# Layout of the stored values: by head instead of by token tile, stored two tiles at a time

## The chip, the cores and the metric

The kernel runs on one core of a Trainium2 chip. The metric is device time in microseconds, the median of several runs. TensorE (PE) multiplies, VectorE (DVE), ScalarE (ACT) and GpSimd (POOL) work on elements, and SyncE (SP) issues nearly all transfers, which sixteen DMA engines carry out.

## The reference

One transformer layer over 2 sequences of 1024 tokens, width 512, 16 heads of 32. Attention and the mixture of experts both read the same normalized input.

```python
xn = _layernorm(x, axis=-1)
Q, K, V = split_heads(xn @ Wq.T), split_heads(xn @ Wk.T), split_heads(xn @ Wv.T)
S = where(causal, einsum('bhqd,bhkd->bhqk', Q, K) * scale, -1e30)
attn = (softmax(S) @ V).transpose(0, 2, 1, 3).reshape(b, t, D) @ Wo.T
routed = sum over the 2 chosen of 8 experts: weight * (silu(xn @ gw.T) * (xn @ uw.T)) @ dw.T
x + attn + routed + shared_mlp(xn)
```

## The kernel before

All of it is one program in five stages, each a block with a barrier between them: the norm stage (`norm_phase`), the projection of queries and keys (`project_phase`), attention with the shared expert mixed in (`attend_phase`), the output projection, and the routed experts. Large products are done in two parts, hi and lo, whose sum is the fp32 number, so that a stored value of one head has 2 * DK = 64 numbers: 32 hi and 32 lo.

**The norm stage** goes over NT = 16 token tiles of 128 rows. For tile t the steps are: load x (L236), statistics on DVE (L271), normalize on DVE (`scale`, L295), transpose on PE (L386), hi and lo parts of the transposed tile on ACT (L357) and DVE (`lo`, L304), 12 matmuls with the value weights into `ps_v` (L397), hi part of the values on ACT (`v_hi`, L369) and lo part on DVE (`v_lo`, L317), both into `v_stage`, and the store of `v_stage` to memory (`store_v`, L246). The normalized tile is stored too (`store_xn`, L241).

There are four slots for each buffer. The order on each engine is fixed by `pipeline`, which takes a list of (lag, step): in turn t the engine does each step for tile t - lag, in the order of the list. DVE does in one turn invert (lag 1), statistics (0), scale (1), lo (2), aggregate (0), v_lo (4), add_eps (0), save_lo (2). SyncE's list is:

```python
pipeline(sp, NT, U, [(0, load), (0, store_zeros), (3, store_xn), (5, store_v)])
```

So SyncE issues, in turn t, the load of x tile t, the store of normalized tile t - 3, and the store of values of tile t - 5. Each waits for its semaphore, and whatever comes later on SyncE waits behind it. All go to one hardware queue (q1 in the profile), which is a ring on each of the sixteen DMA engines.

`v_hi` waits until the slot that it overwrites has been stored. At the head of the projection stage ACT waits, before its first instruction (L515), until every store of values and of normalized rows has landed.

**Memory layout.** Values go to `v_rows`, of shape [128 partitions, 16 tiles, 16 heads, 64]. The store of a tile is 4096 contiguous bytes for each partition. In the attention stage `load_values` (L939) fetches for each of the 32 (head, sequence) pairs 8 tiles of one head: 8 pieces of 256 bytes for each partition, 4096 bytes apart in memory, which land in `vs` with a gap of two numbers between tiles. `vs` has four slots, and the load for one pair is issued a whole head before PE multiplies with it.

Of the kernel before, what the change touches and what calls it, by code (L numbers as in the profile page):

```python
# [22 lines left out]
F32 = mybir.dt.float32  # L23
# [9 lines left out]
H, DK = 16, 32  # L33
P = 128
# [52 lines left out]
def moe_attention_kernel(nc, x, wqk, wv, wo, router, bias, gate, up, down, sgate, sup, sdown, out):  # L87
    qk_hi = nc.dram_tensor("qk_hi", [2 * D, T], F32, kind="Internal").ap()
    qk_lo = nc.dram_tensor("qk_lo", [2 * D, T], F32, kind="Internal").ap()
    v_dram = nc.dram_tensor("v_rows", [P, NT, H, 2 * DK], F32, kind="Internal").ap()  # L90
    row_dram = nc.dram_tensor("max_rows", [2 * H, S], F32, kind="Internal").ap()
    xn_dram = nc.dram_tensor("xn_rows", [T + P, D], F32, kind="Internal").ap()
    slots_dram = nc.dram_tensor("slots", [NSLOT, 2], F32, kind="Internal").ap()
    xt_dram = nc.dram_tensor("xt_blocks", [NTB, P, 2, KC, TBW], F32, kind="Internal").ap()
    with ExitStack() as ctx:
        ident = ctx.enter_context(nc.sbuf_tensor("ident", [P, P], F32))

        slot_of = ctx.enter_context(nc.sbuf_tensor("slot_of", [P, NT, 2], I32))
        entry = ctx.enter_context(nc.sbuf_tensor("entry", [P, NT, 2, 2], F32))

        slot_table = ctx.enter_context(nc.sbuf_tensor("slot_table", [P, NST, 2], F32))
        expert_of = ctx.enter_context(nc.sbuf_tensor("expert_of", [P, NST], I32))


        work = ctx.enter_context(nc.sbuf_tensor("work", [P, NT, D], F32))
        r_hi = ctx.enter_context(nc.sbuf_tensor("r_hi", [P, KC, E], F32R))
        r_lo = ctx.enter_context(nc.sbuf_tensor("r_lo", [P, KC, E], F32R))

        def counters(name, n):
            return [ctx.enter_context(nc.semaphore(f"{name}{k}")) for k in range(n)]  # L110

        v_stored = counters("v_stored", NORM_SLOTS)
        xn_stored = counters("xn_stored", NORM_SLOTS)
        (zeros_stored,) = counters("edge_stored", 1)
        qk_stored = counters("qk_stored", 2)
        (xt_stored,) = counters("xt_stored", 1)
        y_stored = counters("y_stored", YS)

        rows = ctx.enter_context(nc.sbuf_tensor("rows", [P, ROW_SLOTS], I32))
        rows_ready, experts_ready = counters("routed_input", 2)  # L120
        gathered = counters("gathered", GS)
        expert_loaded = counters("expert_loaded", len(FIRST_AT))
        (passed,) = counters("passed", 1)
        with ExitStack() as shared_ctx:

            shared_w = [tuple(shared_ctx.enter_context(nc.sbuf_tensor(name + part, shape, F32R))
                              for part in ("_hi", "_lo"))
                        for name, shape in (("sg", [P, KC, F]), ("su", [P, KC, F]),
                                            ("sd", [P, len(FCH), D]))]
            chosen, weight, earlier_of = [  # L130
                shared_ctx.enter_context(nc.sbuf_tensor(name, [P, NT, E], F32))
                for name in ("chosen", "weight", "earlier_of")]
            count_of = shared_ctx.enter_context(nc.sbuf_tensor("count_of", [P, 1, E], F32))
            with nc.sbuf_tensor("xt_hi", [P, KC, T], F32R) as xt_hi, \
                    nc.sbuf_tensor("xt_lo", [P, KC, T], F32R) as xt_lo:
                norm_phase(nc, x, wv, xt_hi, xt_lo, ident, v_dram, xn_dram, out, work, v_stored,
                           xn_stored, zeros_stored, router, r_hi, r_lo, passed)
                project_phase(nc, wqk, r_hi, r_lo, bias, xt_hi, xt_lo, ident, chosen, weight,
                              earlier_of, count_of, shared_w, sgate, sup, sdown, qk_hi, qk_lo, work,
                              v_stored + xn_stored, zeros_stored, qk_stored, xt_dram, xt_stored)  # L140
            attend_phase(nc, x, ident, qk_hi, qk_lo, v_dram, row_dram, xt_dram, shared_w, sgate,
                         sup, sdown, chosen, weight, earlier_of, count_of, slot_of, entry,
                         slot_table, expert_of, slots_dram, out, work, qk_stored, xt_stored)

        with nc.sbuf_tensor("gu_sb", [P, E * KC, 2 * F], F32) as gu_sb, \
                nc.sbuf_tensor("d_sb", [P, E * len(FCH), D], F32) as d_sb, \
                nc.sbuf_tensor("y_tile", [P, YS, D], F32) as y_tile:
            out_phase(nc, wo, gate, up, down, ident, work, gu_sb, d_sb, out, y_tile, y_stored,
                      slot_table, rows, rows_ready, xn_dram, gathered, passed, expert_loaded)
            routed_phase(nc, gate, up, down, ident, gu_sb, d_sb, slot_table, expert_of, xn_dram,  # L150
                         work, out, y_stored, rows, rows_ready, gathered, passed, expert_loaded,
                         experts_ready)
# [25 lines left out]
def norm_phase(nc, x, wv, xt_hi, xt_lo, ident, v_dram, xn_dram, out, work, v_stored,  # L178
               xn_stored, zeros_stored, router, r_hi, r_lo, passed):

    with ExitStack() as ctx:
# [15 lines left out]
        wv_hi = sbuf("wv_hi", [P, KC, D], F32R)  # L197
        wv_lo = sbuf("wv_lo", [P, KC, D], F32R)
        v_stage = work[:, 0:v_rows, :].bitcast(F32R).rearrange(
            "p (u a) (h d) -> p u (a h) d", u=U, d=2 * DK)  # L200
        ps_t = [psum(f"ps_t{n}", [P, KC, P]) for n in range(U)]
        ps_v = [psum(f"ps_v{n}", [P, D]) for n in range(U)]
        x_loaded = [sem(f"x_loaded{n}") for n in range(U)]
# [24 lines left out]
        with nc.Block() as block:  # L228
            @block.sync
            def _(sp):  # L230
                def load(i, c):
                    t = U * i + c
                    if isinstance(i, int) and i == 0 and c == U - 1:
                        sp.dma_start(wv_raw[:, :, :], wv).then_inc(wv_loaded, 16)
                    wait(sp, xn_ready, t - U + 1)
                    sp.dma_start(x_tile[:, c, :], x[bass.ds(t * P, P), :]).then_inc(x_loaded[c], 16)  # L236

                def store_xn(i, c):
                    t = U * i + c
                    wait(sp, xn_ready, t + 1)  # L240
                    sp.dma_start(xn_dram[bass.ds(t * P, P), :], xn[:, c, :]).then_inc(xn_stored[c], 16)  # L241

                def store_v(i, c):
                    t = U * i + c
                    wait(sp, v_lo_ready, t + 1)
                    sp.dma_start(v_dram[:, bass.ds(t, 1)].rearrange("p a h d -> p (a h) d"),  # L246
                                 v_stage[:, c].bitcast(F32)).then_inc(v_stored[c], 16)

                def store_zeros(i, c):

                    if isinstance(i, int) and i == 1 and c == 0:
                        sp.wait_ge(zeros_ready, 1)
                        sp.dma_start(xn_dram[T:, :], zeros).then_inc(zeros_stored, 16)
                        sp.dma_start(out[T:, :], zeros).then_inc(zeros_stored, 16)
                        sp.dma_start(r_raw[:, :, :], router).then_inc(r_loaded, 16)

                pipeline(sp, NT, U, [(0, load), (0, store_zeros), (3, store_xn), (5, store_v)])
# [10 lines left out]
            def _(dve):  # L268
# [44 lines left out]
                def v_lo(i, c):  # L313
                    t = U * i + c
                    wait(dve, v_hi_ready, t + 1)
                    v = v_stage[:, c]
                    nc.vector.tensor_tensor(v[:, :, DK:], ps_v[c][:, :].rearrange("p (h d) -> p h d", h=H),  # L317
                                            v[:, :, 0:DK].bitcast(F32),
                                            ALU.subtract).then_inc(v_lo_ready, 1)
# [19 lines left out]
            def _(act):  # L339
# [25 lines left out]
                def v_hi(i, c):  # L365
                    t = U * i + c
                    wait(act, v_done, t + 1)
                    wait(act, v_stored[c], 16 * i)
                    nc.scalar.activation(v_stage[:, c, :, 0:DK],  # L369
                                         ps_v[c][:, :].rearrange("p (h d) -> p h d", h=H),  # L370
                                         ACT.Copy).then_inc(v_hi_ready, 1)

# [343 lines left out]
def attend_phase(nc, x, ident, q_hi, q_lo, v_dram, row_dram, xt_dram, shared_w, sgate, sup, sdown,  # L716
# [99 lines left out]
    with ExitStack() as ctx:  # L816
# [104 lines left out]
        with nc.Block() as block:  # L921
            @block.sync
            def _(sp):
# [12 lines left out]
                def load_values(g):  # L936
                    c, h, b = g % HS, g // B, g % B
                    wait(sp, pv_done, NB * (g - HS + 1))
                    sp.dma_start(vs[:, c, :, 0:2 * DK].bitcast(F32),  # L939
                                 v_dram[:, b * QT:(b + 1) * QT, h, :]).then_inc(values_loaded[c], 16)  # L940

                def load_xt(unit):

# [983 lines left out]
```

## Time and profile before

| | us |
|---|---|
| median of 3 runs | 1207.72 |
| lowest and highest | 1205.24, 1207.85 |
| the profiled execution's own time | 1202.2 |
| its span, first to last instruction | 1200.5 |
| PE busy in the span | 1094.9 (91%) |
| DVE busy | 770.7 (64%) |
| DMA queue q1, share of 16 engines | 41.0% |

Times of the trace are counted from the start of the span. The norm stage takes the first 69 us, the projection stage the time to 185 us, attention to about 810 us, and the output projection and the experts the rest.

### The profile page before, as it was taken

What the parts mean: (1) busy time and instruction counts of PE and PEld (TensorE: products, weight loads), DVE (VectorE), ACT (ScalarE), POOL (GpSimd) and SP (SyncE); (2) the same over time, 40 slices, a digit from 0 to 9 for tenths busy, and PEclk for the clock granted to TensorE, in tenths of its full rate; (3) what the DMA queues carried; (4) which work ended last, traced back from release to release, by engine and by line L of the source; (5) the groups of instructions that cost most, each with busy time, mean ns of one, the idle gap of its engine ahead of it and who ended that gap; (6) DMA issues with size and microseconds to landing.
All of it is one profiled execution on the core that took longest, in us unless ns stands there. A gap on an engine that the chain in (4) does not pass through costs nothing. (4 is left out here: it accounts for less than half of the span.)

```text
span 1200.5 us, 19543 instructions
## 1 busy us (share of the span) xinstructions
PE 1094.9 (91%) x5635; PEld 847.7 (71%) x5636; DVE 770.7 (64%) x1473; ACT 639.9 (53%) x1291; POOL 511.3 (43%) x565
## 2 busy tenths in 40 slices
PE   6979994978999999999999999996978999999994
PEld 4848873756677777777777777765867777777773
DVE  6812324645667778877777777644466787788772
ACT  4522220445667667777667766762144555555551
POOL 0018205379655455555555555551003333333331
PEclk9999995988999999999999999997989999999998
DMA  6979549687145264443434336006886433334342
GB/s 213 307 275 353 212 171 199 132 127 136 38 140 141 52 196 102 133 115 71 140 108 141 97 92 191 20 36 219 279 311 176 70 70 70 69 70 70 71 71 35
DMA packets 104648, 165.71 MB, mean 138 GB/s; under 512 B 49040, under 2 KB 59600, under 8 KB 101360
## 3 DMA queue, kind: packets, MB, share of 16 engines
q1 hardware_dynamic: 94128, 143.88, 41.0%
q0 software_dynamic: 9856, 20.53, 9.7%
q8 instruction: 40, 0.66, 0.2%
q10 hardware_dynamic: 576, 0.26, 0.1%
q14 instruction: 48, 0.39, 0.1%
HBM read 103.35 MB, written 61.28 MB: 137 GB/s over the span
## 5 line engine op out<-in xcount | busy, mean ns | idle before, releaser
L1148 POOL TENSOR_TENSOR prob_lo<-prob,prob_hi 128x512 fp32r<-128x512 f32 (+2 forms) x320 | 311.7, 977 | 257.7 <-ACT prob_hi L1197 170.5
L1258 DVE TENSOR_REDUCE maxima<-ps_m 128x1 f32<-128x512 f32 (+3 forms) x384 | 208.4, 553 | 142.8 <-PE ps_m L1378 95.6
L1197 ACT ACTIVATE prob_hi<-prob 128x512 fp32r<-128x512 f32 (+3 forms) x384 | 200.0, 521 | 31.6 <-PE ps_o L1427 18.2
L1190 ACT ACTIVATE prob<-ps_s 128x512 f32<-128x512 f32 (+3 forms) x384 | 185.7, 484 | 28.6 <-POOL prob_lo L1148 23.7
L1814 DVE TENSOR_TENSOR rw_lo<-gu_sb,rw_hi 128x704 fp32r<-128x704 f32 x156 | 139.0, 893 | 47.8 <-ACT rw_hi L1749 43.7
L1728 POOL DMA_INDIRECT out<-work,rows x39 | 61.7, 1582 | 242.8 <-DVE rows L1775 117.6
L1402 PE MATMUL ps_s<-qs,ks 97*128 97x512 f32 (+3 forms) x384 | 148.5, 387 | 14.6 <-ACT prob L1190 12.2
L1375 PE MATMUL ps_m<-ks,qs 96*128 96x512 f32 (+3 forms) x384 | 140.8, 368 | 18.9 <-DMA ks<-qk_hi 17.8
L1749 ACT ACTIVATE rw_hi<-gu_sb 128x704 fp32r x156 | 123.4, 793 | 46.8 <-PE ps_ru L1847 31.8
L1425 PE MATMUL ps_o<-prob_hi,vs 128*66 128x512 f32 (+3 forms) x384 | 133.0, 347 | 1.6 <-POOL prob_lo L1148 1.6
L1427 PE MATMUL ps_o<-prob_lo,vs 128*66 128x512 f32 (+3 forms) x384 | 130.2, 339 | 0.0
L1868 PE MATMUL ps_ry<-d_sb,work 128*128 (+1 forms) x234 | 106.9, 592 | 1.2 <-issue 1.2
L1375 PEld LDWEIGHTS ps_m<-ks,qs 96*128 96x128 f32 x384 | 74.2, 194 | 45.3 <-issue 15.5
L1402 PEld LDWEIGHTS ps_s<-qs,ks 97*128 97x128 f32 x384 | 73.5, 191 | 38.8 <-ACT prob L1190 16.5
L1206 ACT ACTIVATE o_copy<-ps_o 66x512 f32<-66x512 f32 x64 | 38.0, 594 | 117.4 <-PE ps_o L1427 117.4
L1458 PE MATMUL ps_f<-xt,sg_hi 128*128 128x512 f32 (+1 forms) x192 | 74.9, 424 | 8.0 <-DMA xt<-xt_blocks 7.7
L1427 PEld LDWEIGHTS ps_o<-prob_lo,vs 128*66 128x66 f32 x384 | 53.1, 138 | 27.3 <-issue 0.8
L1458 PE MATMUL ps_f<-xt,su_hi 128*128 128x512 f32 (+1 forms) x192 | 70.9, 408 | 0.0
L1868 PEld LDWEIGHTS ps_ry<-d_sb,work 128*128 128x128 f32 (+1 forms) x234 | 43.1, 189 | 38.8 <-issue 38.8
L1740 ACT ACTIVATE xg_hi<-ps_xt 128x512 fp32r<-128x512 f32 x39 | 23.3, 598 | 86.9 <-PE ps_xt L1835 86.9
L1425 PEld LDWEIGHTS ps_o<-prob_hi,vs 128*66 128x66 f32 x384 | 53.1, 138 | 20.9 <-POOL prob_lo L1148 2.2
L1297 DVE TENSOR_TENSOR work<-o_sum,o_inv 128x128 f32<-128x128 f32 x64 | 59.6, 932 | 7.0 <-DVE o_sum L1292 0.5
(210 smaller groups left out, 2430.6 us busy)
## 6 DMA issues: line engine op xcount, KB each, us to landing
xt<-xt_blocks SPq DMA_DIRECT2D x8, 2048.0 KB, 9.2
v_rows<-work SPq DMA_DIRECT2D x16, 512.0 KB, 3.0
qk_hi<-work SPq DMA_DIRECT2D x8, 1024.0 KB, 3.9
qk_lo<-work SPq DMA_DIRECT2D x8, 1024.0 KB, 6.6
qs<-qk_hi SPq DMA_DIRECT2D x64, 128.0 KB, 2.9
ks<-qk_hi SPq DMA_DIRECT2D x64, 128.0 KB, 3.0
vs<-v_rows SPq DMA_DIRECT2D x32, 256.0 KB, 4.6
out<-y_acc SPq DMA_DIRECT2D x32, 256.0 KB
```

The costliest lines, as they stand in the source:

```text
L1148: nc.gpsimd.tensor_tensor(prob_lo[:, s % NPL, 0:w], prob[:, s % NP, 0:w], prob_hi[:, s % NPH, 0:w].bitcast(F32), ALU.subtract).then_inc(lo ...
L1190: nc.scalar.activation(prob[:, s % NP, 0:w], ps_s[s % NS][:, 0:w], ACT.Exp, scale=SCALE).then_inc(exp_done, 1)
L1197: nc.scalar.activation(prob_hi[:, s % NPH, 0:w], prob[:, s % NP, 0:w], ACT.Copy).then_inc(hi_ready, 1)
L1258: nc.vector.reduce_max(maxima[:, c, at:at + 1], ps_m[s % NM][:, 0:w], AX.X).then_inc(m_read, 1)
L1375: last = nc.tensor.matmul(ps_m[s % NM][:, 0:w], qs[0:ROWS, c, t * P:(t + 1) * P], ks[0:ROWS, c, k0:k0 + w], start=True, stop=not diagonal)
L1402: last = nc.tensor.matmul(ps_s[s % NS][:, 0:w], ks[0:ROWS + 1, c, kt * P:(kt + 1) * P], qs[0:ROWS + 1, c, q0:q0 + w], start=True, stop=not ...
L1425: nc.tensor.matmul(into, vs[:, c, kt, :], prob_hi[:, s % NPH, 0:w], start=n in STARTS, stop=False)
L1427: nc.tensor.matmul(into, vs[:, c, kt, :], prob_lo[:, s % NPL, 0:w], start=False, stop=n in ENDS).then_inc(pv_done, 1)
L1458: last = nc.tensor.matmul(ps_f[part][0:w, :], (w_hi, w_lo, w_hi)[term][:, kc, f0:f0 + w], xt[:, (0, 0, 1)[term], kc, :], start=(j == 0), s ...
L1749: nc.scalar.activation(w_hi[:, k, :], chunk(e, k), ACT.Copy).then_inc(w_hi_ready, 1)
L1814: nc.vector.tensor_tensor(w_lo[:, k, :], chunk(e, k), w_hi[:, k, :].bitcast(F32), ALU.subtract).then_inc(w_lo_ready, 1)
L1868: last = nc.tensor.matmul(ps_y[c % 2][:, :], hid_t[0:w, c % HR, k, :], d_sb[0:w, bass.ds(e * NF + k, 1), :].rearrange("p a d -> p (a d)"), ...
```

## The change

The shape of `v_rows` becomes [128 partitions, 16 heads, 16 tiles, 64], so that what a head's load reads is contiguous for each partition (2048 bytes). The stage buffer holds two groups of two tiles, each group laid out as (head, tile, 64). A store is issued after the odd tile of a pair only and carries both tiles: 8 stores of 1 MB in place of 16 of 512 KB. In memory each store writes 512 contiguous bytes for each partition and head. `v_hi` waits for the store of its group, not of its own slot.

```diff
-    v_dram = nc.dram_tensor("v_rows", [P, NT, H, 2 * DK], F32, kind="Internal").ap()
+    v_dram = nc.dram_tensor("v_rows", [P, H, NT, 2 * DK], F32, kind="Internal").ap()
...
-        v_stored = counters("v_stored", NORM_SLOTS)
+        v_stored = counters("v_stored", NORM_SLOTS // 2)
...
-            "p (u a) (h d) -> p u (a h) d", u=U, d=2 * DK)
+            "p (g a) (h u d) -> p g (a h) u d", g=U // 2, u=2, d=2 * DK)
...
                 def store_v(i, c):
                     t = U * i + c
+                    if c % 2 == 0:
+                        return
                     wait(sp, v_lo_ready, t + 1)
-                    sp.dma_start(v_dram[:, bass.ds(t, 1)].rearrange("p a h d -> p (a h) d"),
-                                 v_stage[:, c].bitcast(F32)).then_inc(v_stored[c], 16)
+                    sp.dma_start(v_dram[:, :, bass.ds(t - 1, 2), :], v_stage[:, c // 2].bitcast(F32)
+                                 ).then_inc(v_stored[c // 2], 16)
...
-                    v = v_stage[:, c]
+                    v = v_stage[:, c // 2, :, c % 2]
...
-                    wait(act, v_stored[c], 16 * i)
-                    nc.scalar.activation(v_stage[:, c, :, 0:DK],
+                    wait(act, v_stored[c // 2], 16 * i)
+                    nc.scalar.activation(v_stage[:, c // 2, :, c % 2, 0:DK],
...
-                                 v_dram[:, b * QT:(b + 1) * QT, h, :]).then_inc(values_loaded[c], 16)
+                                 v_dram[:, h, b * QT:(b + 1) * QT, :]).then_inc(values_loaded[c], 16)
```

The order on the other engines is the same as before. On SyncE the rows change in the norm stage alone. Around the first stores of values, before (the three x loads here are those of tiles 5, 6 and 7, the stores of values those of tiles 0, 1 and 2):

```order
L236 DMA x_tile<-in_x 128x512
L241 DMA xn_rows<-work 128x512
L246 DMA v_rows<-work 128x1024
L236 DMA x_tile<-in_x 128x512
L241 DMA xn_rows<-work 128x512
L246 DMA v_rows<-work 128x1024
L236 DMA x_tile<-in_x 128x512
L241 DMA xn_rows<-work 128x512
L246 DMA v_rows<-work 128x1024
```

The same place in the changed program (x loads of tiles 5, 6 and 7; the store carries tiles 0 and 1):

```order
L236 DMA x_tile<-in_x 128x512
L241 DMA xn_rows<-work 128x512
L236 DMA x_tile<-in_x 128x512
L241 DMA xn_rows<-work 128x512
L249 DMA v_rows<-work 2048x1x128
L236 DMA x_tile<-in_x 128x512
L241 DMA xn_rows<-work 128x512
```

The store of one tile has gone from ahead of the load of tile 6, and the load of tile 7 still stands right behind a store, which is now of twice the size and in 2048 rows of 128 numbers instead of 128 rows of 1024. This repeats for each pair: the loads of tiles 7, 9, 11, 13 and 15 stand behind the stores of tiles 0 and 1 to 8 and 9.

At the end of the stage, before (the last three rows together are the stores of tiles 13, 14 and 15):

```order
L241 DMA xn_rows<-work 128x512
L246 DMA v_rows<-work 128x1024
L241 DMA xn_rows<-work 128x512
L246 DMA v_rows<-work 128x1024
L241 DMA xn_rows<-work 128x512
L246 DMA v_rows<-work 128x1024 x3
```

And in the changed program (stores of tiles 10 and 11, 12 and 13, 14 and 15):

```order
L241 DMA xn_rows<-work 128x512
L249 DMA v_rows<-work 2048x1x128
L241 DMA xn_rows<-work 128x512 x2
L249 DMA v_rows<-work 2048x1x128 x2
```

The last store is issued behind the same last step of DVE as before, and carries two tiles. The row of the load of values reads `vs<-v_rows 128x8x64` in both programs: it is still described as 8 pieces of 64 numbers for each partition.

## Rows read from the trace of the kernel before

**Rows 1.** Busy time by stretch (us, busy us and instructions by engine, granted clock, DMA share, GB/s).

```profile
core 0: us, PE busy (x) PEld busy (x) DVE busy (x) ACT busy (x) POOL busy (x), PEclk, DMA share, GB/s
31.00:58.00 27.00, 27.00 (x136) 22.00 (x135) 23.45 (x65) 15.03 (x32) 0.00 (x0) 1.00 0.93 318
500.00:800.00 300.00, 292.92 (x1642) 226.86 (x1641) 209.73 (x427) 210.44 (x487) 165.86 (x170) 1.00 0.37 102
```

**Rows 2.** Waits of 20 to 60 us: total us, times, longest.

```profile
DVE stats L271 <- DMA x_tile<-in_x: 3.7, 9, 0.9
```

**Rows 3.** Timeline of DVE, 37 to 46 us: start, us, what, idle before and releaser.

```profile
37.89 0.66 DVE L317 TENSOR_TENSOR work<-ps_v,work 128x512 fp32r<-128x512 f32 x1
...
40.42 0.68 DVE L304 TENSOR_TENSOR tile_lo<-ps_t,tile_hi 128x512 fp32r<-128x512 f32 x1
...
42.77 0.69 DVE L271 BATCH_NORM_STATS2 stats<-x_tile 128x6 f32<-128x512 f32 x1 [0.51 <-DMA x_tile<-in_x]
...
44.52 0.66 DVE L317 TENSOR_TENSOR work<-ps_v,work 128x512 fp32r<-128x512 f32 x1
```

**Rows 4.** Timeline of SyncE, 38 to 46 us.

```profile
38.72 0.33 SPq L246 DMA_DIRECT2D v_rows<-work  x1
39.26 0.35 SPq L236 DMA_DIRECT2D x_tile<-in_x  x1
39.71 0.67 SPq L241 DMA_DIRECT2D xn_rows<-work  x1
41.93 0.33 SPq L246 DMA_DIRECT2D v_rows<-work  x1
```

**Rows 5.** Timeline of PE, two starts of a tile's twelve matmuls.

```profile
38.18 0.48 PE L397 MATMUL ps_v<-wv_hi,tile_hi 128*128 128x512 f32 x1
...
41.39 0.47 PE L397 MATMUL ps_v<-wv_hi,tile_hi 128*128 128x512 f32 x1
```

**Rows 6.** DMA from 31 to 58 us: packets, and issues with median us to landing.

```profile
DMA packets 3547, 8.58 MB, mean 318 GB/s; under 512 B 389, under 2 KB 389, under 8 KB 3546
...
q1 hardware_dynamic: 3546, 8.56, 93.2%
...
v_rows<-work SPq DMA_DIRECT2D x8, 512.0 KB, 3.0
x_tile<-in_x SPq DMA_DIRECT2D x7, 256.0 KB, 3.4
```

**Rows 7.** DMA from 458.45 to 460.7 us, mostly gate and up weights in pieces of 512 bytes.

```profile
DMA packets 1288, 0.59 MB, mean 261 GB/s; under 512 B 255, under 2 KB 1287, under 8 KB 1287
...
q1 hardware_dynamic: 1271, 0.58, 100.8%
```

**Rows 8.** Issue of the gate weights, SyncE's timeline near 457 us.

```profile
457.01 0.63 SPq L970 DMA_DIRECT2D gu_raw<-in_sup  x1
```

**Rows 9.** DMA issues of the whole span: operation, count, KB each, median us to landing.

```profile
vs<-v_rows SPq DMA_DIRECT2D x32, 256.0 KB, 4.6
...
slots<-slot_table SPq DMA_DIRECT2D x1, 39.0 KB, 18.5
```

**Rows 10.** Timeline of SyncE behind the store of the slot table.

```profile
192.66 0.42 SPq L984 DMA_DIRECT2D slots<-slot_table  x1
193.12 14.60 SPq L957 DMA_DIRECT2D y_acc<-in_x  x4
```

**Rows 11.** Timeline of ACT, 46 to 48 us, and of SyncE and ACT at the end of the stage.

```profile
46.67 0.58 ACT L369 ACTIVATE work<-ps_v 128x512 fp32r<-128x512 f32 x1
...
63.73 4.75 SPq L246 DMA_DIRECT2D v_rows<-work  x3
...
72.33 0.59 ACT L515 ACTIVATE work<-ps_r 8x512 f32<-8x512 f32 x1 [4.82 <-PE ps_r L543]
```

**Rows 12.** Waits of PE for a transfer, 185 to 880 us.

```profile
PE ps_m L1375 <- DMA ks<-qk_hi: 17.8, 2, 13.2
...
PE ps_f L1458 <- DMA xt<-xt_blocks: 7.7, 3, 5.6
```

## The prediction

> **What bounds the kernel now.** I read the stretches first, then the waits, then the timelines of the stretch that the change touches. The stretches say that PE is nearly always busy: 27.00 of 27 us in the middle of the norm stage and 292.92 of 300 us in attention [rows 1]. In the norm stage DVE is busy 23.45 of 27 us and the DMA engines 0.93 of the time at 318 GB/s, in attention only 0.37 [rows 1]. So DMA time is scarce where the stores of values are, and plentiful where their loads are.
>
> The waits say what DVE lacks in the norm stage: the x tile. It waited 9 times between 20 and 60 us, 3.7 us in all [rows 2]. These waits are short, but they are the visible end of a loop that one can follow through two timelines. DVE ends the lo part of a tile's values at 37.89 + 0.66 = 38.55 [rows 3]. SyncE, which was waiting for that, issues the store of values at 38.72 and right behind it the load of x at 39.26 [rows 4]. DVE starts the statistics of that x tile at 42.77, having waited 0.51 us for it, and ends the lo part of the values two tiles on at 44.52 + 0.66 = 45.18 [rows 3]. The loop is thus 4.22 us from lo part to statistics, and 2.41 us from statistics to lo part: 6.63 us for two tiles. PE starts a new tile every 41.39 - 38.18 = 3.21 us [rows 5], 6.42 us for two. Loop and PE are almost equal, and PE has little in reserve: DVE hands over the lo part of the transposed tile at 40.42 + 0.68 = 41.10 [rows 3], and PE wants it at 41.39 [rows 5]. A later x tile costs PE what it is late, less 0.3 us once.
>
> **The change, part by part.** *The store.* Two stores of a tile become one of both. I need the price of a packet. From 31 to 58 us queue q1 took 93.2% of 16 engines in 27 us, 402.6 us of engine time for 8.58 MB [rows 6], or 46.9 ns for 1000 bytes. A packet of 4096 bytes then takes 192 ns; a store of one tile puts 8 of them on each engine, 1.54 us. It lands 3.0 us after its issue [rows 6], so 1.46 us are fixed. The new store has 2048 pieces of 512 bytes, 128 on each engine. No row shows such a store. The nearest is the load of gate and up weights, which is also described as many rows against 128 partitions: 100.8% of 16 engines in 2.25 us for 1271 packets [rows 7], 28.6 ns each, a fifth of them under 512 bytes. I take 30 ns for a piece of 512: 3.84 us on each engine. The issue of that load took 0.63 us [rows 8], against 0.33 for the store now [rows 4], so 0.3 us more. The pair's store lands after 1.46 + 3.84 + 0.3 = 5.6 us, 2.6 us later than one of today.
>
> What counts is what is behind it. The load of tiles 7, 9, 11, 13 and 15 is issued right behind such a store and lands one short transfer after it (39.26 + 3.4 is 42.66, the store 38.72 + 3.0 is 41.72 [rows 4, 6]). If it stands behind the store on each ring, it comes 2.6 us later, five times: 13.0 us. The two-tile loop becomes 9.2 us, and PE, which needs 6.42, waits.
>
> *The other loads.* Those of tiles 6, 8, 10, 12 and 14 lose the wait for the lo part ahead of them, and are issued with the odd one of the pair ahead. They land in time. That ends their own waits of up to half a microsecond, but since the odd loads set the loop it gives nothing.
>
> *Throughput.* A pair now needs 2048 x 30 ns = 61 us for its values and 1.05 MB x 46.9 ns = 49 us for two loads and two stores of rows, 110 us over 16 engines, 6.9 us. That is under 9.2, so the order in the ring decides, not the sum.
>
> *The coarser slot.* ACT overwrites tile 4's slot with tile 8 at 46.67 [rows 11]. The pair of tiles 4 and 5 is stored from 38.72 [rows 4], and lands at 44.3. That leaves 2.3 us, and the late x tile delays ACT as well. Cost nothing; without that cover it would be some microseconds.
>
> *The end of the stage.* The last store is issued at 63.73 + 4.75 - 0.33 = 68.15 [rows 11], behind DVE's last step as before. Today it lands at 71.2, and ACT, which waits for all stores before the router's logits, starts at 72.33 with PE's result [rows 11]. The new one lands at 68.15 + 5.6 = 73.75. PE waits for ACT there: 1.4 us.
>
> *The loads of values.* They are still described as pieces of 64 numbers, so I expect 1024 packets of 256 bytes each as now. A shorter read would be worth something only if someone waited for it. PE's waits for a transfer in attention are for keys (17.8 us, at the start) and for the blocks of x (7.7 us) [rows 12], and no row shows one for values, which land after 4.6 us [rows 9] and are asked for a head later. I count nothing.
>
> The sum is 13.0 + 1.4 = 14.4 us. The profiled execution took 1202.2 us, so 1216.6 in its terms. The median of the runs is 5.5 us above it, 1207.72, and the forecast for the median is 1222.
>
> **Bounds of the unknown price.** Below, a piece costs by its bytes alone, 512 x 46.9 = 24 ns, with no longer issue: landing after 1.46 + 3.07 = 4.5 us, 1.5 later, 7.7 for five and 0.4 at the end, 8.1 us, 1216. Above, by the smallest packets that the trace has. The slot table goes out as 4992 pieces of 8 bytes, 312 on each engine, and lands after 18.5 us [rows 9]: (18.5 - 1.46) / 312 = 55 ns. Then the pair takes 7.0 us on the ring, 5.7 more with the issue, five times 28.8 and 4.6 at the end, 33 us, 1241. The same rows show a ring holding up what follows: the four loads behind that store took 14.60 us to issue [rows 10]. I stay near 30 ns, since those packets are of the very size; scattered writes could be dearer than those reads. With 45 ns it would be 26 us, 1234.
>
> The Trainium skill (DMA: Bandwidth & Descriptors, Specifications) puts the least transfer that still runs at line rate at 512 bytes. By it the new pieces would cost what their bytes cost. The trace disagrees mildly: 28.6 ns for packets of at most 512 bytes is 56 ns for 1000 bytes, against 46.9 for the large ones [rows 6, 7]. What pieces at the price of their bytes would give is the lower bound above, 1216, and I give that case 0.08; the page's rule is what speaks for it.
>
> **Rivals.**
> *Dear writes* (0.17). Each piece goes to another 4096-byte row of memory, and writes may cost 40 to 55 ns. For it: the 55 ns of the slot table, also a scattered write. Against it: most of that may be the price of any tiny packet. 1230 to 1241, most likely about 1234.
> *The load does not stand behind the store* (0.17). If the engines read x while they write values, or if the store drains ahead of time, the odd load lands as now. It decides once it lands within 3.5 us of its issue, as today. The loop then has the slack that the even loads gain, and PE sets the pace: (6.63 - 6.42) x 5 = 1 us less, 1206.7, no change that can be told. For it: bytes in total are the same. Against it: the engines are 0.93 busy with what there is [rows 1], and the loads behind the slot table waited [rows 10].
> *The contiguous read pays* (0.10), the one that ends faster. If the memory serves 2048 contiguous bytes in less time than 8 scattered pieces, each load gives back up to half of its 64 packets at 28.6 ns [rows 7] on an engine, 0.9 us. Where keys or x blocks are waited for (5 waits [rows 12]) that is up to 4.6 us, with the 1 us of the case above up to 5.6: between 1202 and 1206, 1204 as its middle. It decides only if the stores cost nothing as well, and if a load of values is in the ring ahead of what is waited for.
>
> **How the numbers follow.** The forecast's own case, 25 to 40 ns a piece, has 0.48 and spans 1216 to 1230. With pieces by their bytes 0.08, dear writes 0.17, no queueing 0.17 and the paying read 0.10 that makes one. The time is that of the likeliest, 1222. For 8 in 10 the range must reach down to the case without queueing, 1206, and up to 1236; left out are the paying read and the upper third of dear writes. This measurement tells no change within about 0.2%, or 2.4 us. Slower by more: 0.48 + 0.08 + 0.17 = 0.73; no change 0.17; faster 0.10.
>
> **What would show it.** In the changed profile the norm stage should end near 82 us instead of 69; DVE's waits for x tiles should be about 2.5 to 3 us every second tile, five of them; PE's share in that stage should fall; the store of values should land after about 5.6 us and the x loads in two groups, near 6 and under 4. DMA packets under 2 KB should grow by 16384, those under 512 bytes stay. Attention should keep its length. I am wrong in the price if the landing of the store differs, in the queueing if the store lands late and x does not, in the reserve of PE if x lands late and PE doesn't wait, and in the cover of the loads if attention changes.

## The result and the profile after

| | before | after |
|---|---|---|
| median of 8 runs each, us | 1206.74 | 1218.82 |
| lowest and highest | 1202.7, 1211.13 | 1214.85, 1223.31 |
| ratio of after to before | | 1.0102, 95% interval 1.0077 to 1.0127 |
| profiled execution's own time, span | | 1223.31, 1221.6 |

The change costs 12.1 us. The ratios here and below are those on record, with their intervals; they are not the quotients of the two medians, from which some differ by 0.1 or 0.2%. The two profiled executions are 21.1 us apart, because that of before (1202.2 us) is shorter than any of the 8 runs in the table and that of after (1223.31) is the longest of its own. So I compare stretches that the change touches, not the spans.

The waits of after, 20 to 80 us (us in total, times, longest):

```profile
DVE stats L274 <- DMA x_tile<-in_x: 16.6, 5, 3.8
```

Nine short waits, 3.7 us in all [rows 2], have become five long ones. Two turns of DVE (start, us, what, idle before and releaser):

```profile
44.24 0.66 DVE L320 TENSOR_TENSOR work<-ps_v,work 128x512 fp32r<-128x512 f32 x1
...
45.31 0.68 DVE L274 BATCH_NORM_STATS2 stats<-x_tile 128x6 f32<-128x512 f32 x1
...
51.97 0.69 DVE L274 BATCH_NORM_STATS2 stats<-x_tile 128x6 f32<-128x512 f32 x1 [3.77 <-DMA x_tile<-in_x]
...
53.71 0.66 DVE L320 TENSOR_TENSOR work<-ps_v,work 128x512 fp32r<-128x512 f32 x1
```

And SyncE in the same stretch and at the end of the stage:

```profile
45.07 0.57 SPq L249 DMA_DIRECT2D v_rows<-work  x1
45.85 1.74 SPq L236 DMA_DIRECT2D x_tile<-in_x  x1
47.69 1.18 SPq L241 DMA_DIRECT2D xn_rows<-work  x1
49.41 0.34 SPq L236 DMA_DIRECT2D x_tile<-in_x  x1
...
79.26 4.98 SPq L249 DMA_DIRECT2D v_rows<-work  x2
```

The loop of [rows 3, 4] is here with a longer middle. The lo part of an odd tile ends at 44.24 + 0.66 = 44.90, SyncE issues the pair's store at 45.07 and the load of x at 45.85. DVE has that x at 51.97, 7.07 us after the lo part where it was 4.22, and the next odd lo part ends at 54.37. Here that is 9.47 us for a pair. PE's granted clock fell to its lower level in this turn (row 44.30:47.70 below); the next two pairs, without that, took 8.99 each. The even tile's x, used at 45.31, is not waited for. Over five pairs (tiles 1 to 11) the lo parts end at 26.58 and 72.35, 9.15 us for a pair; in the kernel before they end at 24.91 and 58.29 (57.63 + 0.66), 6.68.

Busy time by stretch (us, busy us and instructions by engine, granted clock, DMA share, GB/s), and DMA from 31 to 58 us:

```profile
core 0: us, PE busy (x) PEld busy (x) DVE busy (x) ACT busy (x) POOL busy (x), PEclk, DMA share, GB/s
31.00:58.00 27.00, 22.14 (x98) 17.06 (x97) 17.18 (x48) 11.39 (x25) 0.00 (x0) 0.94 0.74 226
44.30:47.70 3.40, 3.40 (x10) 2.72 (x9) 3.40 (x12) 1.86 (x4) 0.00 (x0) 0.50 0.42 121
71.70:75.10 3.40, 3.40 (x10) 2.68 (x9) 2.93 (x9) 1.86 (x4) 0.00 (x0) 0.51 0.45 126
84.90:88.30 3.40, 3.37 (x9) 1.13 (x10) 0.00 (x0) 0.00 (x0) 0.49 (x2) 0.55 1.01 286
500.00:760.00 260.00, 254.21 (x1428) 198.27 (x1428) 191.24 (x389) 181.50 (x422) 144.65 (x147) 0.99 0.42 119
```

```profile
DMA packets 7527, 6.11 MB, mean 226 GB/s; under 512 B 240, under 2 KB 5989, under 8 KB 7525
...
q1 hardware_dynamic: 7525, 6.09, 73.2%
...
v_rows<-work SPq DMA_DIRECT2D x3, 1024.0 KB, 5.7
```

PE had 136 instructions in these 27 us and has 98, and the DMA engines are less busy than before (0.74 against 0.93 [rows 1]): nothing lacks bandwidth, the work stands in a chain. The price of a 512-byte piece can now be read. q1 took 0.732 x 27 x 16 = 316.2 us of engine time. The 1536 packets over 2 KB are x and normalized rows of 2048 bytes, at 46.9 ns for 1000 bytes [rows 6] 96 ns each, 147.5 us. The other 168.7 us over 5989 - 240 = 5749 pieces are 29.3 ns each. The store lands after 5.7 us.

The packets of the whole execution, in the kernel before and in after, and the landings that the page of after lists:

```profile
DMA packets 104648, 165.71 MB, mean 138 GB/s; under 512 B 49040, under 2 KB 59600, under 8 KB 101360
...
DMA packets 118856, 165.71 MB, mean 136 GB/s; under 512 B 48912, under 2 KB 75856, under 8 KB 115568
...
v_rows<-work SPq DMA_DIRECT2D x8, 1024.0 KB, 5.7
...
vs<-v_rows SPq DMA_DIRECT2D x32, 256.0 KB, 4.7
```

Packets under 2 KB grew by 75856 - 59600 = 16256, and those under 512 bytes went from 49040 to 48912, 128 fewer. The difference, 16384, is the number of the new 512-byte pieces. A load of values lands after 4.7 us, before 4.6 [rows 9].

### The profile page after: what moved, and what is told of

Read it like the earlier page. It is cut to its first block and busy times, and to the rows that moved or that the text cites. A ratio compares the mean times of both kernels' runs of the same rounds, so it can differ in the third digit from the quotient of the medians.

```text
span 1221.6 us, 19526 instructions
## 1 busy us (share of the span) xinstructions
PE 1102.3 (90%) x5635; PEld 849.4 (70%) x5636; DVE 769.3 (63%) x1473; ACT 639.3 (52%) x1291; POOL 509.8 (42%) x565
## 2 busy tenths in 40 slices
DMA packets 118856, 165.71 MB, mean 136 GB/s; under 512 B 48912, under 2 KB 75856, under 8 KB 115568
## 5 line engine op out<-in xcount | busy, mean ns | idle before, releaser
L1378 PE MATMUL ps_m<-ks,qs 96*128 96x512 f32 (+3 forms) x384 | 140.3, 367 | 18.9 <-DMA ks<-qk_hi 17.8
L1871 PEld LDWEIGHTS ps_ry<-d_sb,work 128*128 128x128 f32 (+1 forms) x234 | 43.2, 189 | 38.8 <-issue 38.8
```

What stands on the lines that cost most here:

```text
L1378: last = nc.tensor.matmul(ps_m[s % NM][:, 0:w], qs[0:ROWS, c, t * P:(t + 1) * P], ks[0:ROWS, c, k0:k0 + w], start=True, stop=not diagonal)
L1871: last = nc.tensor.matmul(ps_y[c % 2][:, :], hid_t[0:w, c % HR, k, :], d_sb[0:w, bass.ds(e * NF + k, 1), :].rearrange("p a d -> p (a d)"), ...
```

## Experiments

All times are medians of runs made beside runs of the kernel before on the same chip; e1 to e4, e5 to e7 and e8 to e10 are three such groups, on three chips. "Pair" is the mean time of two tiles on DVE over the five pairs described above.

| kernel | us | before beside it | ratio (95%) | pair, us |
|---|---|---|---|---|
| before | | | | 6.68 |
| after | 1218.82 | 1206.74 | 1.0102 (1.0077 to 1.0127) | 9.15 |
| e1_pairs_tile_layout | 1213.76 | 1208.72 | 1.0048 (1.0024 to 1.0073) | 7.72 |
| e2_by_head_single | 1218.46 | 1208.72 | 1.0089 (1.0051 to 1.0126) | 8.70 |
| e3_after_loads_ahead | 1210.31 | 1208.72 | 1.0009 (0.9976 to 1.0042) | 6.49 |
| e4_before_loads_ahead | 1209.9 | 1208.72 | 0.9993 (0.9962 to 1.0024) | 6.47 |
| e5_after_act_ring | 1223.7 | 1207.55 | 1.0133 (1.0105 to 1.016) | 9.21 |
| e6_after_split_store | 1208.29 | 1207.55 | 1.001 (0.9987 to 1.0033) | 7.14 |
| e7_before_no_value_loads | 1206.89 | 1207.55 | 0.9994 (0.9968 to 1.002) | 6.69 |
| e8_act_ring_same_time | 1223.25 | 1211.12 | 1.0092 (1.0065 to 1.0118) | 9.21 |
| e9_act_ring_no_wait | 1210.72 | 1211.12 | 1.0006 (0.998 to 1.0031) | 6.47 |
| e10_store_twice | 1247.48 | 1211.12 | 1.0319 (1.0273 to 1.0366) | 12.66 |

### Each half of the change alone

**Pairs in the old layout.** The kernel before, with one store for two tiles: one run of 8192 bytes for a partition. As in the changed kernel, `v_hi` waits for the store of its pair.

```diff
-                    sp.dma_start(v_dram[:, bass.ds(t, 1)]..., v_stage[:, c]...).then_inc(v_stored[c], 16)
+                    if c % 2 == 0:
+                        return
+                    sp.dma_start(v_dram[:, bass.ds(t - 1, 2)]..., v_stage[:, c - 1:c + 1]...
+                                 ).then_inc(v_stored[c // 2], 16)
```

> The kernel before with the pairing alone: one store for two tiles, in the old layout, so 8192 contiguous bytes for each partition. Ring theory (an x load comes late by what the store ahead of it takes on the ring): 3.07 us on each engine, store lands after 4.5 us, loop of two tiles 8.2 us instead of 6.67, norm stage 7 to 9 us longer, ratio to before 1.006 to 1.008. Rival (only the small pieces cost): store lands after 3 us or x is not late, stage as before, ratio 1.000. Rival (pairing is all of it, pieces cost by their bytes): as the changed kernel, loop 9.2 us, ratio 1.010.

Its waits of 20 to 80 us, its transfers of 31 to 58 us, and ACT at the head of the projection stage:

```profile
DVE stats L274 <- DMA x_tile<-in_x: 9.5, 5, 2.0
ACT work L518 <- DMA v_rows<-work: 5.0, 1, 5.0
```

```profile
v_rows<-work SPq DMA_DIRECT2D x4, 1024.0 KB, 4.5
x_tile<-in_x SPq DMA_DIRECT2D x6, 256.0 KB, 4.5
```

```profile
79.57 0.59 ACT L518 ACTIVATE work<-ps_r 8x512 f32<-8x512 f32 x1 [4.97 <-DMA v_rows<-work]
```

The store lands 1.5 us later than one of a single tile. Its 8 packets on each engine have 8192 bytes instead of 4096, 1.54 us more at the rate of [rows 6]. A pair takes 7.72 us, 1.04 longer than in the kernel before; I had expected 8.2. In the middle of the stage the x tile lands 0.6 us behind the store here, where it lands 1.1 us behind a store of one tile in the kernel before, so a part of the delay is got back. Pairing thus costs by itself, with the bytes unchanged and half the packets for the values: 5.0 us of the median. The last row shows the wait for the last store: PE has the first result at 78.56 + 0.40 = 78.96, ACT takes it at 79.57, 0.6 us later.

**By head, one tile at a time.** The kernel before with the new shape of `v_rows` and of the load of values: 16 stores of 2048 pieces of 256 bytes.

```diff
-    v_dram = nc.dram_tensor("v_rows", [P, NT, H, 2 * DK], F32, kind="Internal").ap()
+    v_dram = nc.dram_tensor("v_rows", [P, H, NT, 2 * DK], F32, kind="Internal").ap()
...
-                    sp.dma_start(v_dram[:, bass.ds(t, 1)].rearrange("p a h d -> p (a h) d"),
+                    sp.dma_start(v_dram[:, :, bass.ds(t, 1), :].rearrange("p h a d -> p h (a d)"),
```

> The kernel before with the layout alone: 16 stores of one tile, each in 2048 pieces of 256 bytes (128 on each engine). Ring theory: the store lands 1.46 + 128 x 25 ns = 4.7 us after issue, x loads 1.7 us late, every one of them. The engines' sum is 4096 pieces x 25 ns + 49 us for two tiles, 9.4 us over 16 engines, so here the sum binds before the order does: loop 9.4 us, norm stage 13 to 15 us longer, ratio 1.011 to 1.013. Rival (only the order behind the store counts): loop 8.3 us, ratio 1.007. Rival (bytes alone count): as before, 1.000.

DMA from 31 to 58 us, and the wait of 20 to 80 us:

```profile
DMA packets 14607, 6.50 MB, mean 241 GB/s; under 512 B 13032, under 2 KB 13032, under 8 KB 14606
...
q1 hardware_dynamic: 14606, 6.48, 97.0%
...
v_rows<-work SPq DMA_DIRECT2D x6, 512.0 KB, 4.8
```

```profile
DVE stats L271 <- DMA x_tile<-in_x: 14.4, 9, 2.5
```

Here every x load stands behind a store, nine are waited for, and the engines are full: 0.970 x 432 = 419.0 us, less 1574 packets of 96 ns, over 13032 is 20.6 ns for a piece of 256 bytes. (The 13032 include the few hundred smaller packets that the other windows show as well, 389 in [rows 6]; without 300 of them it would be 21.0.) I had said 25, and from it 9.4 us for a pair, where it takes 8.70. With 20.6 a pair of tiles needs 2 x 128 x 20.6 ns + 32 x 96 ns = 8.3 us on each engine, and one takes 8.25 to 8.5 once the first is over. The sum of the engines' work and the chain give nearly the same here, so this run doesn't tell which of them sets its pace. It does show that the layout alone loses as much as the whole change to within the measurement (1.0089 against 1.0102). Against it, after moves the same bytes in half the pieces, each store in place of two, and its pair still takes longer (9.15), since twice as much stands ahead of the load that sets the loop.

### Is it the place behind the store?

**Loads a turn ahead of the store.** In SyncE's list the store's lag goes from 5 to 6. Each load of x is then issued before the store that it stood behind, which comes a turn later. Done to after and to before.

```diff
-                pipeline(sp, NT, U, [(0, load), (0, store_zeros), (3, store_xn), (5, store_v)])
+                pipeline(sp, NT, U, [(0, load), (0, store_zeros), (3, store_xn), (6, store_v)])
```

> The changed kernel with SyncE's stores of values one turn later in its list, so that each x load is issued a turn ahead of where it stood (3.2 us or more). Same transfers and sizes. Ring theory: stores still land after 5.7 us, but no x load is waited for; the loop goes to PE's 6.42 us or the engines' sum of 6.9 us; norm stage 12 to 14 us shorter than in the changed kernel, ratio to before 1.000 to 1.003. Rival (the engines' sum or the coarser slot of v_stage binds): no better than the changed kernel, 1.010.

> The same reordering in the kernel before. Loop theory (x loads and PE are nearly equal): DVE's waits for x tiles vanish, two tiles take 6.42 instead of 6.67 us, stage 1 to 1.5 us shorter, ratio 0.998 to 1.000. Rival (DVE's waits cost nothing because PE alone sets the pace): no change of the stage at all.

After with the loads ahead: its busy time, the wait of 20 to 80 us, and its transfers of 31 to 58 us:

```profile
26.00:58.00 32.00, 32.00 (x161) 26.25 (x160) 28.40 (x79) 19.00 (x40) 0.00 (x0) 1.00 0.97 295
```

```profile
DVE stats L274 <- DMA x_tile<-in_x: 2.6, 4, 0.9
```

```profile
DMA packets 10697, 8.49 MB, mean 314 GB/s; under 512 B 323, under 2 KB 8642, under 8 KB 10695
...
q1 hardware_dynamic: 10695, 8.47, 101.4%
...
v_rows<-work SPq DMA_DIRECT2D x4, 1024.0 KB, 6.5
```

The same 512-byte pieces, even slower to land, and PE is busy 32.00 of 32 us. The whole loss of the stage is gone: a pair takes 6.49, and from the lo part of tile 1 to that of tile 15 it is 43.0 us, in the kernel before 43.2 and in after 57.1. The total is within measurement of before. The price again: 1.014 x 432 = 438.0 us, less 2053 packets of 96 ns, over 8319 pieces is 29.0 ns. The engines are then full: PE's pace and theirs meet. In the kernel before the same edit ends DVE's waits for x altogether, and a pair takes 6.47, PE's own 6.42 [rows 5]. That is 1 us over five pairs, but the last four tiles take 10.67 us instead of 9.83, so that from tile 1 to tile 15 only 0.2 us is gained. DVE's short waits in the kernel before cost next to nothing.

**Half of the store behind the load.** The pair's store in two halves by heads. The first 8 heads are stored where the store was, the other 8 behind the load of x.

```diff
-                    sp.dma_start(v_dram[:, :, bass.ds(t - 1, 2), :], v_stage[:, c // 2]...
+                    sp.dma_start(v_dram[:, 0:H // 2, bass.ds(t - 1, 2), :], v_stage[:, c // 2, 0:H // 2]...
+                def store_rest(i, c): ...    # heads H // 2 to H
...
+                pipeline(sp, NT, U, [(0, load), (0, store_zeros), (6, store_rest), (3, store_xn), (5, store_v)])
```

> The changed kernel with each pair's store cut in two by heads (8 and 8): the first half ahead of the x load, the second behind it. Same pieces of 512 bytes and same bytes. Ring theory: 64 pieces on each engine ahead of the odd load, 1.9 us instead of 3.84, x 0.4 to 0.8 us later than before; loop 7.1 to 7.5 us, norm stage 2 to 5 us longer than before, ratio 1.002 to 1.004. Rival (what counts is the engines' sum or the kind of write, not what is ahead of the load): as the changed kernel, loop 9.2 us, 1.010.

Its wait of 20 to 80 us, and its transfers of 31 to 58 us:

```profile
DVE stats L282 <- DMA x_tile<-in_x: 6.2, 7, 1.6
```

```profile
v_rows<-work SPq DMA_DIRECT2D x8, 512.0 KB, 3.8
x_tile<-in_x SPq DMA_DIRECT2D x7, 256.0 KB, 3.9
```

With 64 pieces instead of 128 ahead of the load on each engine, a pair takes 7.14 in place of 9.15. 64 x 29.3 ns is 1.88 us; 2.01 were saved, with one issue more. What stands ahead of the load counts, not the pieces in total. The 0.46 us for a pair that are left would be 2.3 over five; in the total no change can be told (1.001, 0.9987 to 1.0033).

**The store twice.** After, each pair's store is done to `v_rows` and once more to another array, both ahead of the load.

```diff
+                    for n in range(2):
+                        sp.dma_start(v_dram[n][:, :, bass.ds(t - 1, 2), :], v_stage[:, c // 2]...
```

> The changed kernel with every pair stored twice, the second time to another tensor that nothing reads: 256 pieces of 512 bytes on each engine ahead of the odd x load. Ring theory: 3.8 to 4.3 us more for each pair, loop 13.0 to 13.6 us against 9.16, norm stage 20 us longer than in the changed kernel, ratio to before 1.026 to 1.030. Rival (the delay does not grow with what is ahead of the load): loop 9.2 us, ratio 1.010.

SyncE and DVE in one turn:

```profile
38.55 0.58 SPq L251 DMA_DIRECT2D v_rows<-work  x1
39.23 1.72 SPq L251 DMA_DIRECT2D v_copy<-work  x1
41.23 3.45 SPq L237 DMA_DIRECT2D x_tile<-in_x  x1
```

```profile
48.67 0.69 DVE L276 BATCH_NORM_STATS2 stats<-x_tile 128x6 f32<-128x512 f32 x1 [6.96 <-DMA x_tile<-in_x]
```

A pair takes 12.66, 3.51 more for 128 pieces more on each engine, 27.4 ns each; I had expected 13.0 or more. DVE's wait grew from 3.77 to 6.96. The five pairs account for 17.5 us of the 24 us by which this kernel lies above after (36.4 us above the kernel before beside it, after 12.1). Most of the rest is at the end of the stage, where ACT now waits for the copy:

```profile
115.07 0.59 ACT L521 ACTIVATE work<-ps_r 8x512 f32<-8x512 f32 x1 [14.40 <-DMA v_copy<-work]
```

DVE's last lo part ends at 101.28, 13.8 us earlier; in after it ends at 83.68, 5.9 us before ACT starts.

### Is it the ring, or the engines?

**The store on ACT's ring, at its old lag.** SyncE's list loses the store; ACT issues it after `v_hi` at lag 5, on its own queue (q10).

```diff
-                pipeline(act, NT, U, [(0, root), (1, hi), (1, split_wv), (1, save_hi), (3, v_hi)])
+                pipeline(act, NT, U, [(0, root), (1, hi), (1, split_wv), (1, save_hi), (3, v_hi), (5, store_v)])
```

> The changed kernel with the stores of values issued by ScalarE instead of SyncE, at the same lag, so that they sit on another queue's ring of the same engines. Ring theory (first come first served within one queue's ring): x loads no longer stand behind the store, only share the engines with it, and are late by at most 1 us; stage 10 us or more shorter than in the changed kernel, ratio to before 1.000 to 1.004. Rival (the engines serve packets in order of issue whatever the ring, or the writes themselves block): x late by 2.6 us as in the changed kernel, ratio 1.010.

ACT in one turn, and its wait of 20 to 80 us:

```profile
38.66 0.60 ACT L372 ACTIVATE work<-ps_v 128x512 fp32r<-128x512 f32 x1 [5.12 <-DMA v_rows<-work]
...
41.43 0.59 ACTq L381 DMA_DIRECT2D v_rows<-work  x1
```

```profile
ACT work L372 <- DMA v_rows<-work: 19.1, 5, 5.1
```

No load of x is waited for any more, and the kernel is slower still. ACT comes to the store last in its turn: the first store leaves 4.6 us after the lo part that it carries, the next four 7 to 10 us after it, and they land after 6 to 9 us. `v_hi` of the pair that reuses the slots waits for it, and DVE and PE behind it; the waiting `v_hi` also stands ahead of the next store. This is the coarser slot of the prediction without its cover: 16 us in the total. As a test of the ring it says nothing.

**The store on ACT's ring, as early as it can go.** The same with the store at lag 4, right behind `root`, so that it stands ahead of ACT's long steps. Nothing keeps the x loads behind it.

> As e5 (stores on ScalarE's ring, x loads free of them), but each store issued within 1 us of the lo part instead of 4 us after it. If what made e5 slow was the coarser slot (ScalarE waiting 16.2 us for a store to land before it overwrites the group), these waits vanish and the stage is that of e3: loop 6.4 to 6.9 us, ratio to before 1.000 to 1.003. Rival (the second ring itself is slow): loop 8 us or more, ratio 1.007 to 1.013.

No wait of DVE for x and none of ACT for a store is left, and a pair takes 6.47. So the loss of the run before was the slot. Again this doesn't test the ring, since the x loads run ahead.

**The same, with the load at its old time.** Each odd x load on SyncE's ring now waits for the hi part of the tile three back (`wait(sp, hi_ready, t - 2)`, met once t - 2 hi parts are done), which puts it some 1.4 us behind the store on ACT's ring, 0.6 to 0.7 us later than it is in after. SyncE's loop is written out in full for this (`back=NT`).

> The changed kernel with the pair's store on ScalarE's ring, issued within 1 us of the lo part that it waits for, and the odd x load made to wait until ScalarE has issued it (for the hi part of the next tile), so it is issued last as in the changed kernel, some 0.8 us later than there, but on another ring. Ring theory (first come first served within one queue's ring, packets of two rings served in turn): x lands 3.5 to 4.5 us after its issue although the store takes 5.7 or more; loop 7.8 to 8.6 us. Rival (an engine works off what was issued first on any ring): x lands 5.3 us or more after its issue, loop 9.5 to 10 us.

ACT's queue, SyncE's queue and DVE in one turn, and all DMA packets from 46.2 to 49.7 us:

```profile
44.70 0.57 ACTq L383 DMA_DIRECT2D v_rows<-work  x1
```

```profile
46.11 0.33 SPq L238 DMA_DIRECT2D x_tile<-in_x  x1
```

```profile
51.07 0.69 DVE L276 BATCH_NORM_STATS2 stats<-x_tile 128x6 f32<-128x512 f32 x1 [2.57 <-DMA x_tile<-in_x]
```

```profile
DMA packets 1766, 0.90 MB, mean 258 GB/s; under 512 B 0, under 2 KB 1766, under 8 KB 1766
...
q10 hardware_dynamic: 1766, 0.90, 99.2%
```

The store lands at 50.48, the x tile at 51.05. It has its own ring and still comes 4.9 us after its issue and 0.6 us behind the store, where it took 3.4 in the kernel before [rows 6]. The pair takes 9.21, as in after. Both lie between what I had set down for the two theories (landing within 4.5 us and a pair of at most 8.6, against 5.3 or more and at least 9.5), so the times alone do not decide. The packets do: the x load was issued at 46.11, and from 46.2 to 49.7 all 1766 packets were the store's, on ACT's queue q10, and none was of q1. The load does not stand behind the store in a ring alone: the x load had to wait until the store was nearly through, though it had come by the other queue. Whether it waited in the sixteen engines, or where the transfers are cut into packets for them, is not shown.

The Trainium skill (DMA: Bandwidth & Descriptors, Queues, rings and completion order) says that each engine goes round its queues and takes a packet of several descriptors from each in turn. By that the load, with few descriptors on each engine, would have come through the store early; this trace does not agree, with no packet of q1 for 3.5 us while q10 was served, 4.9 us from issue to landing, and the load landing 0.6 to 1.0 us behind the store in every turn.

### The loads of values

**Only the first four loads of values.** The kernel before, with the loads of later heads left out (28 of 32), so that attention multiplies with the first values all along.

```diff
-                    wait(sp, pv_done, NB * (g - HS + 1))
+                    if g >= HS:
+                        return
...
-                        pe.wait_ge(values_loaded[c], 16 * (g // HS + 1))
+                        pe.wait_ge(values_loaded[c], 16)
```

> The kernel before without the loads of values after the first four (heads 2 and on multiply with the values of the first four pairs; that part of the result is left wrong in value, all other work stays). It bounds what a cheaper read of values could give. Hidden-load theory: no change of attention, ratio 0.998 to 1.001. Rival (the read is worth something to keys and x blocks): 4 to 5 us faster, 0.996.

Attention from 500 to 760 us, without the loads and then in the kernel before; and, from the kernel without them, a stretch at the head of the projection stage:

```profile
500.00:760.00 260.00, 254.77 (x1441) 198.96 (x1440) 189.58 (x388) 181.44 (x422) 142.26 (x147) 1.00 0.34 105
...
71.00:74.40 3.40, 3.39 (x10) 1.14 (x11) 0.00 (x0) 0.00 (x0) 0.47 (x2) 0.59 0.60 186
```

```profile
500.00:760.00 260.00, 254.54 (x1438) 198.67 (x1438) 189.80 (x388) 182.27 (x423) 144.16 (x148) 1.00 0.42 116
```

The DMA share falls from 0.42 to 0.34, PE stays busy 254.8 of 260 us against 254.5, and the total doesn't move (0.9994, 0.9968 to 1.002). No saving on the loads of values, however large, can make this kernel faster by more than that measurement tells, 0.3%.

## Why the prediction was right, step by step

**The loop** was right. The store was to land after 5.6 us and lands after 5.7; the pair was to take 9.2 us and takes 9.15. Five odd loads were to cost 13.0; the stretch from tile 1 to tile 11 grew by 45.77 - 33.38 = 12.4. Without the clock's fall it would have been less: the last two pairs took 8.99 each, with x 6.6 us behind the lo part, 2.3 later than the 4.2 of [rows 3], and not 2.6. Moving the loads ahead of the same store takes it all away, splitting the store takes most of it, and doubling it adds what its pieces cost.

**The price of a piece**, 30 ns taken from a load of weights, is 29.3 and 29.0 ns by the busy time of the engines and 27.4 by the doubled store. Scattered writes are no dearer than those reads, and the *dear writes* fall. *By bytes alone* (24 ns, 1216 us) falls too: after and e1 write the same bytes, and a pair takes 9.15 against 7.72. The Trainium skill's line rate at 512 bytes (DMA: Bandwidth & Descriptors, Specifications) would make these two alike; the trace shows 29 ns for 512 bytes where a large packet's rate gives 24.

**The other loads** gained nothing, as said. They land 4.1 to 5.3 us after their issue and not under 4, and are not waited for.

**Throughput** was right: 0.74 of the engines is in use in after, and 1.01 where the loads are ahead. The 6.9 us that the sum gave for a pair was 0.4 too much: in e3 the engines do a pair in 6.49.

**The coarser slot** cost nothing, as said, and "some microseconds" without its cover was right in kind: the store 4.6 to 10 us behind its lo part (e5) turned it into five waits of up to 5.1 us, 19.1 in all. The cover is thin.

**The end of the stage**, 1.4 us, is not shown in this profile. The last store lands at 89.4, and ACT starts at 89.55, where it waited for PE:

```profile
89.55 0.59 ACT L518 ACTIVATE work<-ps_r 8x512 f32<-8x512 f32 x1 [6.48 <-PE ps_r L546]
```

PE ran at a granted clock of 0.55 there (row 84.90:88.30 above), near its lower level of 1.2 GHz, after 2.6 us of idling at the barrier, and hid the store's lateness. e7, which has the stores of before, shows the same dip (0.59), as do ten of the twelve profiles; only the profiled execution of before and that of e1 do not. So this dip is not of the change, and the term counts in full only in executions without it. e1's profile has it as 0.6 us, for a store that takes 4.2 us to land instead of 5.7. For after itself an estimate: in e1 PE's first result came 2.95 us after its first matmul (76.01), and 2.95 from 84.93 is 87.88. ACT would then have waited for the store until 89.36, 1.5 us.

**The clock** is a term that the prediction does not have. Inside the norm stage the granted clock fell to its lower level in after (at 44.3 and 71.6), e2, e5, e8 and e10. In these five PE's longest idle stretch of the stage is 1.8 to 4.9 us (2.2 in after); in the seven other profiles it is at most 0.9, and the clock, once up (at 17 to 21 us), never falls there. In after the pair with the first fall took 9.47 us; of the four without one the first took 9.35 and the other three 8.97 to 8.99. The last four tiles are 1.5 us slower in after (11.3 us against 9.8), with a granted clock of 0.51 from 71.7 to 75.1; e2, e6 and e8, without a fall there, took 9.8 too, while e3, e4 and e9, whose pairs are shorter, took 10.6 to 10.7 without one. So a part of the loss goes by the clock, as an estimate from these differences some 0.5 and up to 1.5 us in this one profile. How much of it is in the median of eight runs is not shown.

**The loads of values** and **attention** were right. PE's waits for keys were 17.8 us as in [rows 12], those for blocks of x 6.4 against 7.7, and e7 shows that their cover is complete. *The contiguous read pays* falls with it.

**The load does not stand behind the store** fell as a rival, and e8 shows more than I had argued: I had put the queueing in the ring, and it holds across two queues.

The sum of 14.4 us stands against 12.1 measured, with an interval from 9.3 to 15.3 (0.77 to 1.27% of 1206.74). The loop's 12.4 us are seen in the profile; the 1.4 us at the end of the stage are not, and falls of the clock that the sum did not have stand beside them. That the terms come so near the median is thus in part luck. Of the forecast's 1222 us a further 1 us came from the median of the three runs at hand, 1207.72, where eight gave 1206.74.

## What to carry to other kernels

Price a transfer by what stands behind it in the DMA engines, not by its own bytes: the loads that an engine will wait for belong ahead of a long store with many pieces, and another issuing engine's queue did not move them ahead here. Fewer issues are no gain by themselves, since the next load waits for the whole of a store of twice the size, and a buffer that is freed in groups needs its store early. Before making a read cheaper, take it out and see whether the time moves.

## What the runs showed of the hardware

A load issued on SyncE's ring 1.4 us after a store of 128 pieces on each engine on ACT's ring landed 0.6 us behind that store, 4.9 us after its issue, and none of its packets moved while the store's did from 46.2 to 49.7 us (e8). Pieces of 256 bytes took 20.6 ns each (e2) and pieces of 512 bytes 29 (after, e3), where packets of 4096 take 192 [rows 6]: half the piece costs 0.7 of the time. Behind a long store an issue is slow itself: 1.74 us for the x load in after, 3.45 behind the doubled store, against 0.35 before [rows 4]. TensorE's granted clock fell to its lower level (0.50, row 44.30:47.70) inside the norm stage in the five profiles in which late transfers left PE idle for 1.8 to 4.9 us at the longest, and in none of the seven with at most 0.9.
